# Attention scores from two float32r parts instead of three bf16 parts, two heads beside each other on the rows of the array, maxima read from two PSUM banks and one in turn

## What is computed

```python
h = emb[x]                                   # x: 2 x 2048 token numbers, D_MODEL 256
Q, K, V = (heads(wq, bq), heads(wk, bk), heads(wv, bv))   # 16 heads of 16
score = jnp.einsum('bhsd,bhtd->bhst', Q, K) / jnp.sqrt(jnp.float32(D_K))
attn = jax.nn.softmax(score, axis=-1)
o = jnp.einsum('bhst,bhtd->bhsd', attn, V)
```

## Time and profile before

| | us |
|---|---|
| median of three runs | 3946.2 |
| profiled execution | 3942.12 |
| its span | 3940.3 |
| attention, first load to last value matmul | 132 to 1685 |
| TensorE busy in the whole span | 3642.9 (92%) |
| VectorE | 2970.8 (75%) |
| ScalarE | 2765.8 (70%) |

### The profile page before, as it was taken

One profiled execution on the slowest core, in us unless ns is written; L12 is line 12 of the kernel. 1 busy time (PEld: TensorE's weight loads), 2 busy tenths in 40 slices (PEclk: granted clock), 3 DMA queues, 4 the chain that ended last, 5 costly groups with the idle time before them and its releaser, 6 DMA issues. The chain is left out here.

```text
span 3940.3 us, 64166 instructions
## 1 busy us (share of the span) xinstructions
PE 3642.9 (92%) x20577; PEld 1970.5 (50%) x20577; DVE 2970.8 (75%) x3944; ACT 2765.8 (70%) x3830; POOL 1451.6 (37%) x1284
## 2 busy tenths in 40 slices
PE   7699999999999999945899999999999999996999
PEld 4223333233323333222677767777777777775554
DVE  5799999899989999333778888888888888886111
ACT  2246666666666666812888999999888989996232
POOL 3000000000000000000677877777777877786000
PEclk9789999999999999977999999999999999998999
DMA  5510101010100100042011111111111111113221
GB/s 136 150 42 4 41 4 41 4 42 16 30 22 23 38 7 4 5 138 81 33 44 55 60 55 55 59 63 53 52 47 54 60 55 55 49 55 102 81 92 49
DMA packets 121702, 202.32 MB, mean 51 GB/s; under 512 B 25392, under 2 KB 68368, under 8 KB 121456
## 3 DMA queue, kind: packets, MB, share of 16 engines
q1 hardware_dynamic: 101264, 173.97, 13.7%
q10 hardware_dynamic: 18656, 20.85, 1.7%
q0 software_dynamic: 1536, 4.20, 0.7%
HBM read 147.83 MB, written 50.72 MB: 50 GB/s over the span
## 5 line engine op out<-in xcount | busy, mean ns | idle before, releaser
L1047 POOL TENSOR_TENSOR m_g<-m_hs,m_cb 128x512 f32<-128x512 f32 x1024 | 1295.4, 1280 | 379.3 <-DVE m_hs L1322 376.3
L661 DVE TENSOR_REDUCE a_mx<-a_ps_m 128x1 f32<-128x512 f32 x2048 | 1311.8, 686 | 156.4 <-PE a_ps_m L520 139.2
L632 ACT ACTIVATE a_probs<-a_ps_s 128x1024 f32<-128x1024 f32 x1024 | 995.0, 1020 | 466.5 <-PE a_ps_s L557 465.9
L1322 DVE TENSOR_TENSOR_SCAN m_hs<-m_da,m_carry,m_ps_x 128x512 f32<-128x512 f32 x768 | 967.8, 1274 | 177.8 <-PE m_ps_x L1118 157.1
L1248 ACT ACTIVATE m_da<-m_delta,m_a_cur 128x512 f32<-128x512 f32 x1024 | 734.0, 717 | 102.1 <-DVE m_hs L1322 101.2
L520 PE MATMUL a_ps_m<-a_k,a_q 112*128 112x512 bf16 x2048 | 732.0, 394 | 41.9 <-DMA a_q<-q_scr 26.5
L1233 ACT ACTIVATE m_bu<-m_dut,m_bt 128x512 f32<-128x512 f32 x1024 | 730.8, 714 | 0.2
L1118 PEld LDWEIGHTS m_ps_x<-m_ident,m_bu 128*128 128x128 f32 x4096 | 494.6, 144 | 383.4 <-issue 302.0
L1118 PE MATMUL m_ps_x<-m_ident,m_bu 128*128 128x128 f32 x4096 | 635.0, 278 | 41.8 <-DVE m_hs L1322 28.8
L1130 PE MATMUL m_ps_y<-m_ident,m_g 128*128 128x128 f32 x4096 | 625.5, 276 | 14.0 <-POOL m_g L1047 14.0
L557 PE MATMUL a_ps_s<-a_q,a_k 115*128 115x512 bf16 (+1 forms) x2048 | 611.3, 381 | 1.4
(11 more groups left out here) (154 smaller groups left out, 2461.4 us busy)
## 6 DMA issues: line engine op xcount, KB each, us to landing
m_cb<-c_scr SPq DMA_DIRECT2D x128, 512.0 KB, 3.7
y_scr<-m_ysb SPq DMA_DIRECT2D x16, 1024.0 KB, 6.7
ffn_y<-y_scr SPq DMA_DIRECT2D x16, 1024.0 KB, 10.2
a_k<-k_scr SPq DMA_DIRECT2D x224, 64.0 KB, 2.2
a_q<-q_scr SPq DMA_DIRECT2D x224, 64.0 KB, 2.6
m_xn<-xn_scr SPq DMA_DIRECT2D x16, 512.0 KB, 5.1
q_scr<-p_partsq SPq DMA_DIRECT2D x24, 256.0 KB, 2.4
k_scr<-p_partsk SPq DMA_DIRECT2D x24, 256.0 KB, 2.6
```

What stands on the lines that cost most here:

```text
L632: nc.scalar.activation(probs[:, t % 2, 2 * half:2 * half + 2], ps_s[half][:, :, :], ACT.Exp, scale=float(DK) ** -0.5).then_inc(exped, 1)
L661: nc.vector.reduce_max(mx[:, i // NC, i % NC:i % NC + 1], bank(i), AX.X).then_inc(m_maxed, 1)
L1047: nc.gpsimd.tensor_tensor(g[:, t % NG], hs[:, t % NHS], cb[:, quarter % 2, n % CQ], ALU.mult).then_inc(g_ok, 1)
L1322: nc.vector.tensor_tensor_scan(hs[:, t % NHS, rev], da[:, t % NDA, rev], ps_x[:, t % NX, rev], carry[:, n, i:i + 1] if p else 0.0, ALU.mul ...
```

## The change

- q and k are kept in two float32r parts instead of three bf16 parts. ScalarE writes the first part with the bias, VectorE makes the second from PSUM with one operation for each half. Three products instead of seven make a score: 48 rows of the array, and two rows more for the parts of the negative maximum.
- Two heads stand side by side: one on the rows from 0, one on the rows from 64. Blocks of the maxima alternate between the two.
- The three banks of `ps_m` are filled in rounds of banks 0, 1 and 2. VectorE reduces banks 0 and 1 in one operation and bank 2 in another: 22 rounds, 42 operations for a chunk instead of 64. Rounds 4 and 21 don't use bank 2; in round 4 it holds the transposed maxima.
- On TensorE two blocks of the maxima and two score matmuls alternate; POOL's four operations become one, after ScalarE's copy. The inner loops over chunks on TensorE are unrolled.

```diff
-Q_PART = [0, 0, 1, 1, 0, 2, 1]
-K_PART = [0, 1, 0, 1, 2, 0, 2]
+Q_PART = [0, 0, 1]
+K_PART = [0, 1, 0]
...
-                        nc.vector.tensor_copy(part[0], full[a][:, :, :]).then_inc(step, 1)
-                        nc.vector.tensor_tensor(rest[:, :, :], full[a][:, :, :], part[0], ALU.subtract).then_inc(step, 1)
-                        nc.vector.tensor_copy(part[1], rest[:, :, :]).then_inc(step, 1)
-                        nc.vector.tensor_tensor(part[2], rest[:, :, :], part[1], ALU.subtract).then_inc(parts_ok[a], 1)
+                        for m in range(KD):
+                            last = nc.vector.scalar_tensor_tensor(
+                                out=parts[a][:, buf, 1, m], in0=ps_qk[a][:, m], scalar=b_col[a][:, m:m + 1],
+                                in1=parts[a][:, buf, 0, m].bitcast(FP32), op0=ALU.add, op1=ALU.subtract)
...
+        NEG = 4
+        ROUNDS = BLK // 3 + 1
+        FREE = (NEG, ROUNDS - 1)
+        slots = [(r, b) for r in range(ROUNDS) for b in range(3) if b < 2 or r not in FREE]
+        ops = [(r, b) for r, b in slots if b != 1]
...
                 def max_blocks(m, buf, c, first, end, loads=None):
                     for i in range(first, end):
+                        pair, st, tc, half = i // 32, i // 8 % 4, i // 2 % 4, i % 2
+                        row = half * (P // 2)
+                        r, b = slots[i]
+                        if b < 2:
+                            pe.wait_ge(m_maxed, ONE + m * OPS + maxed(r - 1, 0))
                         else:
+                            pe.wait_ge(m_maxed, ONE + m * OPS + maxed(r - 2 if (r - 1) % ROUNDS in FREE else r - 1, 2))
+                            if r - 1 == NEG:
+                                pe.wait_ge(neg_h, ONE + m)
+                        nc.tensor.matmul(ps_m[:, b], q_st[row:row + KQ, buf, c, pair, st * P:(st + 1) * P],
+                                         k_st[row:row + KQ, buf, pair, tc * CH:(tc + 1) * CH],
                                          start=True, stop=True).then_inc(m_scored, 1)
...
                     for t in range(NT):
-                        maximum()
+                        maxima(2)
                         for half in range(2):
                             for i in range(2):
+                                row = i * (P // 2)
+                                last = nc.tensor.matmul(ps_s[half][:, i], k_st[row:row + KQM, buf, half, t * P:(t + 1) * P],
+                                                        q_st[row:row + KQM, buf, c, half],
                                                         start=True, stop=True)
-                                if i == half:
-                                    maximum()
+                            if half == 0:
+                                maxima(2)
-                        maximum()
                         if t > 0 or v_buf is not None:
                             values(v_buf if t == 0 else buf, (t - 1) % NT)
...
                 def maxima(m):
-                    for i in range(BLK):
-                        nc.vector.reduce_max(mx[:, i // NC, i % NC:i % NC + 1], bank(i), AX.X).then_inc(m_maxed, 1)
+                    for j, (r, b) in enumerate(ops):
+                        i = slots.index((r, b))
+                        wide = 2 if b == 0 else 1
+                        dve.wait_ge(m_scored, ONE + m * BLK + i + wide)
+                        nc.vector.reduce_max(mx[:, i:i + wide], ps_m[:, b:b + wide], AX.X).then_inc(m_maxed, 1)
```

More of the change, by code:

```diff
@@ L6 @@
 FP32 = mybir.dt.float32
-BF16 = mybir.dt.bfloat16
+F32R = mybir.dt.float32r
 I32 = mybir.dt.int32
@@ L20 @@
 G = B * H // HG
[L21 to L24 removed]
+HP = HG // 2
+PARTS = 2
+Q_PART = [0, 0, 1]
+K_PART = [0, 1, 0]
 KQ = DK * len(Q_PART)
@@ L37 @@
 FF, RK = 1024, 64
-TWO_BF16_ONES = float(np.array([0x3F803F80], np.uint32).view(np.float32)[0])
 ONE = 1
@@ L93, in embed_and_project @@
         hT = sb("p_hT", [P, 2, KD, CH], FP32)
-        full = [sb(f"p_full{n}", [P, KD, CH], FP32) for n in "qk"]
-        rest = sb("p_rest", [P, KD, CH], FP32)
-        parts = [sb(f"p_parts{n}", [P, 2, PARTS, KD, CH], BF16) for n in "qk"]
+        parts = [sb(f"p_parts{n}", [P, 2, PARTS, KD, CH], F32R) for n in "qk"]
         ps_t = pb("p_ps_t", [P, KD, CH], FP32)
@@ L402, in load @@
                     for h in heads:
+                        first, pair = h % 2 * (P // 2), h // 2
                         for stack, scr, part in ((k_st, k_scr, K_PART), (q_st, q_scr, Q_PART)):
@@ L498, in body @@
                         stage_v(g + 1, 1 - buf)
-                    with pool.Fori(AHEAD, NC if last else NC + AHEAD) as c:
-                        split(g * NC + c)
+                    with pool.Fori(1, NC if last else NC + 1) as c:
+                        low(g * NC + c)
                 groups(pool, body)
@@ L520, in max_blocks @@
-                        nc.tensor.matmul(bank(i), q_st[0:KQ, buf, bass.ds(c, 1), h, st * P:(st + 1) * P].rearrange("p c n -> p (c n)"),
-                                         k_st[0:KQ, buf, h, tc * CH:(tc + 1) * CH],
+                        pair, st, tc, half = i // 32, i // 8 % 4, i // 2 % 4, i % 2
+                        row = half * (P // 2)
+                        if i % 32 < 2 and loads is not None:
+                            pe.wait_ge(loaded[buf][2 * pair + half], ONE + loads)
+                        r, b = slots[i]
@@ L541, in chunk, with maxima @@
                     e = g * NC + c
-                    pe.wait_ge(neg_in, ONE + 16 * PARTS * (e + 1))
+                    pe.wait_ge(neg_in, ONE + 32 * PARTS * (e + 1))
                     taken = 0
-                    def maximum():
+                    def maxima(count):
                         nonlocal taken
@@ L594, in body @@
                     chunk(g, buf, 0, None if first else 1 - buf, buf, AHEAD, True)
-                    with pe.Fori(1, NC - AHEAD) as c:
+                    for c in range(1, NC - AHEAD):
                         chunk(g, buf, c, buf, buf, c + AHEAD, True)
                     if last:
-                        with pe.Fori(NC - AHEAD, NC - 1) as c:
+                        for c in range(NC - AHEAD, NC - 1):
                             chunk(g, buf, c, buf, None, None, True)
@@ L601, in body @@
                     else:
-                        with pe.Fori(NC - AHEAD, NC) as c:
+                        for c in range(NC - AHEAD, NC):
                             chunk(g, buf, c, buf, 1 - buf, c - (NC - AHEAD), True)
```

173 lines of the change are left out of this document (67 added, 106 removed).

## The result

The changed kernel takes 4264.5 us (median of four runs, 4254.6 to 4284.4), the kernel before, run beside it, 3943.3 (3939.9 to 3947.3). The ratio is 1.082, with a 95% interval of 1.078 to 1.087. The forecast was 4078: slower, as forecast, and inside the wide range of 3880 to 4330, but outside the forecast's own range of 4045 to 4135: the loss is 321 us where about 132 was worked out. The profiled execution took 4271.3 (span 4269.5).

The account below looks back on a forecast made before the run. TensorE was taken to bound the steady part, VectorE 0.24 us behind. 3942.12 + 130 (steady chunks) + 9 (first maxima) - 3 (projection) - 4 (end) = 4074, median 4078 us; own range 4045 to 4135, wide 3880 to 4330.

Parts of the forecast that it names:

- banks b0 and b1 are reduced together, so neither can be written while that reduce runs: Attention's steady part: only b2 gives slack, 0.60 us, against 0.49 less 0.08 for rewriting both banks.
- the order written out from it: Steady part, TensorE's fixed order: three turns take 9.19 us, with weight loads 9.34, or 3.11 a turn instead of 2.84.
- The interpolated price of a reduce of two banks: VectorE in the attention: 1.22 us recorded, the next reduce 1.14 after it, taken from 256- and 1024-element operations.
- the term for weight loads: Exposed loads on TensorE in the steady part: 0.03 us each (0 to 0.1), 0.15 per three turns.
- rival 3: TensorE falls to its lower clock in the attention: 4750 us if throughout, 4300 and more if in turns; chance 0.10.
- Its sign, a granted clock under 0.95 in the attention: The observation in the attention that would show TensorE had fallen to its lower clock.
- what was forecast as +6: Ahead of the steady part: maxima of the first two chunks +9 us together, the projection -3.
- Rival 1: Attention: held matmuls don't delay the others, VectorE bounds at 38.0 us a chunk; 3717 us, or about 3857; chance 0.18.
- Rival 2: Attention: a pair's matmuls run one after the other, or float32r passes cost twice bf16's; +166, 4245 us; chance 0.11.
- Rival 4: Attention: float32r matmuls cost what float32 ones do, 4.5 us a turn at the least, 4750 and more; chance 0.02.
- Projection -3: End of the projection: fewer VectorE operations on q and k let the last stores end near 127; 3 us saved.
- End -4: Last two chunks, without maxima: pairs save at most 0.18 us in each of 32 turns; taken as 4 us saved.

Follow-up runs that it names:

- experiment 2: The changed kernel with q, k and the negative maximum in two bf16 parts instead of float32r: 4074.1 us, ratio 1.033.
- Experiment 3: The kernel before with only the reduce of banks 0 and 1 in one operation (42 reduces a chunk) added: 4188.3 us, ratio 1.062.
- experiment 1: The changed kernel with 64 single-bank reduces over three banks in turn, TensorE's order kept: 4149.6 us, ratio 1.052.
- experiment 7: The changed kernel with two more, overwritten score matmuls in each turn ahead of the second pair of maxima: 4210.6 us, ratio 1.068.
- experiment 10: The kernel before with its maxima and scores on 66 rows instead of 112 and 115, same instructions and order: 4745.8, 4795.3, 5200.4 and 5211.8 us.
- experiment 9: The changed kernel with bf16 parts instead of float32r and both heads of a pair on the rows from 0: 5308.0 us, ratio 1.347.
- experiment 6: The changed kernel with single-bank reduces, one block of maxima behind each half of the scores, and bf16 parts instead of float32r: 3797.3 us, ratio 0.963.
- experiment 4: The changed kernel, float32r kept, with both heads of a pair on the rows from 0: 5480.4 us, ratio 1.390.
- experiment 5: The changed kernel with single-bank reduces and one block of maxima behind each half of the scores, float32r kept: 3912.4 us, ratio 0.993.
- experiment 8: The changed kernel with the second pair of maxima moved behind the second half of the scores, two-bank reduces kept: 4129.6 us, ratio 1.048.

## Why the prediction was right in direction and wrong in size

**The mechanism held, for the wait between the two engines.** The step "banks b0 and b1 are reduced together, so neither can be written while that reduce runs" and the order written out from it were right to 0.1 us in three turns: 9.19 without weight loads, (49.70 - 0.25)/16 x 3 = 9.27 with bf16 parts (experiment 2). Experiment 3 shows such a loss without anything else of the change, experiment 1 the gain of undoing it. The interpolated price of a reduce of two banks held too: with the single one behind it it takes 1.82 us (644.70), where the forecast's prices give 1.14 + 0.69.

**The step that failed is the term for weight loads**: "0 to 0.1 on each such matmul or pair, about five of which lie on the path of three turns. I take 0.03 each". Three turns of the median chunk take (53.47 - 0.25)/16 x 3 = 9.98, so the five places cost 9.98 - 9.19 = 0.79, or 0.16 each, above even the upper bound of 0.1. The load of 48 rows in float32r lasts 0.18 (the row of 644.13 above), longer than the float32 load of 128 rows (0.14) from which I bounded it; where TensorE has waited it isn't hidden. The term was +24. Without loads a chunk is 16 x 9.19/3 + 0.25 = 49.26, so it is 30 x (53.47 - 49.26) = +126; experiment 2 puts 113 of it to float32r in place of bf16. That inside float32r it is the load, and not something else of the format, rests on the records (0.50 behind an exposed load, 0.40 behind a hidden one) and not on a run of its own.

**The second step that failed is the clock, which the sum put at nothing.** Held as rival 3, it came true in part, on top of the forecast and not in its place. I gave it 0.10 and priced it at 4300 and more; it acts in a few chunks (+66, experiment 7) and ahead of the loop. Its sign, a granted clock under 0.95 in the attention, was met (0.51 from 380 to 400). Ahead of the loop the forecast priced the first chunk at full clock among the transposes, since the earlier trace rows showed 1.00 in that stretch. It ran at 0.50 (1.34 from M to M instead of 0.44), and a float32r matmul behind an exposed load is recorded at 1.2 GHz with 0.79 where I had 0.61 from bf16. This makes +33 us of what was forecast as +6 (the projection's -3 in it). With bf16 parts (experiment 2) the same stretch is also at 0.50, and the first chunk ends at 201.13 and the second takes 43.18: 16 of the 33 come without float32r, 17 with it. The low clock there has more than one way in: from 170 to 187 experiment 1's kernel is at 0.50 with TensorE busy 17.00 of 17 us, so it didn't wait, and experiment 3's, with all 112 rows, at 0.70 with waits. What I missed is a thing that the earlier trace rows could not show: I compared the new turn's busy share (56%) with stretches that used 112 rows or more (37% and 73%), and in experiment 10 TensorE was busy 300 of 300 us on 66 rows at 0.50.

The Trainium skill (TensorE: Matmul & The Clock Gate, A second HAM failure mode: psum-queue depth-cycling), cited ahead as not shown, names small idle times between groups of matmuls that go round the PSUM banks as a cause of the clock's going to and fro. The changed kernel's trace agrees: TensorE waits 0.88 and 1.07 us ahead of a block, and its clock goes between 1.00 (300 to 320) and 0.51 (380 to 400). With the wait filled it stays at 1.00 from 300 to 700 (experiment 7). Experiments 1, 9 and 10 show 0.50 with hardly any wait (99.97 of 100 us busy, 298.28 and 300.00 of 300), so waits are not the only cause.

**Rival 1** (VectorE the bound, 38.0 a chunk) is false for this kernel: in the three turns shown VectorE is idle 0.56 + 1.66 = 2.22 us before reduces of two banks (about 1.8 was forecast) and 0.40 before one of a single bank, far over the 0.7 given as the point of decision. Its relief is real though: with the order mended and bf16 parts a chunk takes 40.95 (experiment 6).

**Rival 2** (pairs one after the other): false. The two matmuls of a pair start within 4 ns of each other (804.485 and 804.489 in the changed kernel's trace), recorded together with 0.50, and where no load is exposed the next pair follows 0.23 later (644.47 to 644.70). **Rival 4** (float32r at the price of float32): false; the recorded matmul takes 0.39 to 0.40 when its load is hidden, as the bf16 one does.

**Smaller terms.** Projection -3: the first block of the maxima began 2.5 us earlier (147.12), but its partner waited for more of q until 149.31, so nothing was gained. End -4: -3. The return of the outer loop costs 2.6 us instead of 5.75, which I had left unchanged; the loops over chunks inside are unrolled now, but no run tests that this is why.

**What stays open.** What exactly the granted clock follows. The price of an overlapped and of a serial pair at full clock, since without overlap the clock falls (experiments 4 and 9). Why experiments 5 and 8 have chunks 1.4 to 1.6 above the writing-out: with bf16 parts experiment 6 meets its 41.0, so the excess of experiment 5 belongs to float32r, but that it is the exposed loads is argued, not shown.

## What to carry to other kernels

Before PSUM banks are grouped under one reading operation, write out three or four turns of both engines' orders: a reader that holds two of three banks saved VectorE a third of its reduces and cost 244 us, because TensorE works in a fixed order and scores and values stood behind the held matmul. Relieving an engine gains nothing while the wait that it runs into holds up the work behind it; the same float32r pairs lose 8% with the wide reduces and the paired order, and gain 0.7% with single ones spread out. And look at the granted clock in every stretch after any edit that uses fewer rows of the array or leaves it waiting, also where the busy share is full.

## What the runs showed that was not expected

- The same instructions on 66 rows instead of 112 and 115 run at 1.2 GHz for whole chunks (86.6 us) with TensorE busy 300 of 300, and at 2.4 GHz for others (45.6); on 112 and 115 rows the steady chunks all ran at 2.4 GHz (45.69).
- Two useless matmuls in each turn made the kernel 54 us faster (4264.5 to 4210.6), by holding the clock at 1.00.
- A float32r weight load of 48 rows takes 0.18 us at full clock, a bf16 one 0.10; where it is exposed, the reduce behind it comes 0.14 later and the next pair 0.11.
